# Normalisation in four groups, roots moved to GpSimd, and a new order of the first phase in an attention-and-FFN kernel

## The reference

```python
xn = (x - mean(x)) / sqrt(var(x) + 1e-5)              # by row; f32
Q, K, V = relu(xn @ Wq + bq), relu(xn @ Wk + bk), relu(xn @ Wv + bv)   # 16 heads of 8
s = layernorm(softmax(mask(Q @ K.T / sqrt(8))) @ V + xn) * gamma + beta # causal and key/query masks
xl = (xn - mu) * rsqrt(var(xn) + 1e-5) * ln_scale + ln_bias
xa = xl @ attn_w.T + attn_b + xn
h  = gelu(xa @ w1[e] + b1[e]);  eo = h @ w2[e] + b2[e]  # expert e fixed by the row's place
g = silu(gelu(eo @ next_w.T + next_b))
out = x + s * g
```

## Time and profile before

| | us |
|---|---|
| median of 3 runs | 456.26 |
| the 3 runs | 455.87, 456.26, 466.83 |
| the profiled execution's own time | 457.67 |
| its span, first to last instruction | 455.6 |
| VectorE busy in the span | 373.1 |
| TensorE busy in the span | 383.3 |
| GpSimd busy in the span | 179.1 |

### The profile page before, as it was taken

One profiled execution on the slowest core, in us unless ns is written; L12 is line 12 of the kernel. 1 busy time (PEld: TensorE's weight loads), 2 busy tenths in 40 slices (PEclk: granted clock), 3 DMA queues, 4 the chain that ended last, 5 costly groups with the idle time before them and its releaser, 6 DMA issues.

```text
span 455.6 us, 9692 instructions
## 1 busy us (share of the span) xinstructions
PE 383.3 (84%) x3541; PEld 249.3 (55%) x3541; DVE 373.1 (82%) x865; ACT 289.2 (63%) x580; POOL 179.1 (39%) x446
## 2 busy tenths in 40 slices
PE   0041899889999998899999999999999999999850
PEld 0021575457877775456656656665666566566420
DVE  5899388977778921899899999898999998989427
ACT  0122481278898884167777877877778778778740
POOL 9237000411111002311236547456556383565591
PEclk9997599999999999999999999999999999999995
DMA  8910030077644534723233342423332424340000
GB/s 238 316 52 1 0 100 0 0 170 160 156 112 115 139 98 116 128 57 86 81 90 79 82 109 73 118 63 105 92 96 64 129 56 113 79 110 27 4 24 23
DMA packets 31413, 41.72 MB, mean 92 GB/s; under 512 B 5910, under 2 KB 23686, under 8 KB 31366
## 3 DMA queue, kind: packets, MB, share of 16 engines
q1 hardware_dynamic: 31206, 41.08, 34.6%
q0 software_dynamic: 160, 0.03, 0.0%
HBM read 26.43 MB, written 11.02 MB: 82 GB/s over the span
## 4 chain that ended last, share of the span: by engine, by line
PE 43%; DVE 13%; issue 2%; ACT 1%; POOL 1%; DVEq 0%; ACTq 0%; POOLq 0%
PE banks L1152 15%; PE banks L1135 8%; DVE mx L951 8%; PE banks L1115 8%; PE banks L1117 5%; PE banks L1137 5%; DVE stats L996 2%; PE banks L1162 2%; DVE res L990 1%; ACT pt L1070 1%; PE banks L1124 0%; DVE res L977 0%; DVE res L980 0%; DVE mixed L981 0%; DVE aggr L1000 0%
## 5 line engine op out<-in xcount | busy, mean ns | idle before, releaser
L951 DVE TENSOR_REDUCE mx<-banks 128x1 f32<-128x512 f32 (+3 forms) x352 | 200.0, 633 | 19.9 <-PE banks L1117 18.2
L1070 ACT ACTIVATE pt<-banks 128x512 f32<-128x512 f32 x320 | 169.2, 601 | 44.2 <-PE banks L1137 36.7
L1152 PE MATMUL banks<-pt,vg 128*18 128x512 f32 (+3 forms) x1024 | 81.4, 436 | 0.7 <-ACT pt L1070 0.7
L1115 PE MATMUL banks<-k_own,q_own 76*128 76x384 bf16 (+2 forms) x192 | 48.4, 274 | 5.4 <-DVE mx L951 2.7
L1115 PE MATMUL banks<-w_room 76*128 76x384 bf16 (+2 forms) x192 | 48.1, 274 | 3.3 <-DVE mx L951 3.3
L842 POOL TENSOR_SCALAR mneg<-mx 128x16 f32<-128x16 f32 x32 | 8.1, 254 | 107.7 <-DVE mx L951 106.6
L1135 PE MATMUL banks<-w_room 76*128 76x384 bf16 (+2 forms) x192 | 47.5, 275 | 0.9 <-ACT pt L1070 0.5
L1135 PE MATMUL banks<-q_own,k_own 76*128 76x384 bf16 (+2 forms) x192 | 47.8, 274 | 0.0
L1152 PEld LDWEIGHTS banks<-pt,vg 128*18 128x18 f32 x1024 | 23.7, 97 | 43.8 <-issue 33.4
L1117 PE MATMUL banks<-k_own,q_own 124*128 124x128 bf16 x256 | 44.0, 219 | 0.0
L1117 PE MATMUL banks<-w_room 124*128 124x128 bf16 x256 | 43.8, 219 | 0.0
(11 more groups left out here) (175 smaller groups left out, 764.3 us busy)
## 6 DMA issues: line engine op xcount, KB each, us to landing
k_scratch<-parts SPq DMA_DIRECT2D x40, 128.0 KB, 2.4
k_own<-k_scratch SPq DMA_DIRECT2D x48, 96.0 KB
w_room<-k_scratch SPq DMA_DIRECT2D x48, 96.0 KB
q_scratch<-parts SPq DMA_DIRECT2D x24, 128.0 KB, 2.4
q_own<-q_scratch SPq DMA_DIRECT2D x32, 96.0 KB
w_room<-q_scratch SPq DMA_DIRECT2D x32, 96.0 KB
w_room<-in_w_dram SPq DMA_DIRECT2D x1, 2048.0 KB, 9.1
q_own<-q_scratch SPq DMA_DIRECT2D x16, 112.0 KB
```

Of the source, the lines that this page charges most:

```text
L951: dve.tensor_reduce(mx[:, u % 2, heads[0]:heads[-1] + 1, q], banks[:, S0 + slots[0] % SLOTS, 0:w * len(heads)].rearrange("p (h k) -> p h k ...
L1070: act.activation(pt[:, T * j:T * j + T], banks[:, bank(), :], ACT.Exp, scale=SCALE).then_inc(exp_done, 1)
L1115: mm(o[:, 0:w - P], qx[by][0:LIVE, g, h, P * q:P * q + P], kx[by][0:LIVE, g, h, 0:w - P], start=True, stop=True)
L1152: ins = mm(banks[32 * h:32 * h + VP, OT, P * k:T], vg[:, g, k, h, :], pt[:, KPLACE[k, h]:KPLACE[k, h] + n], start=(k == 0 and g % 2 == 0), ...
```

## The change

1. `GROUPS` becomes four groups of eight row tiles, which is two batches each. The DMAs of x stay two.
2. VectorE computes the roots of group 0 as before. For groups 1 to 3 it computes `statistics` (mean, variance, first seed of the root), GpSimd computes the roots (`first_roots`, 31 instructions of eight columns), and VectorE takes the inverse (`inverses`).
3. VectorE's order becomes: for each batch quotients, sums and the rests of the batch before; the statistics of groups 1, 2 and 3 follow the sums of batches 0, 2 and 4. The low parts of batch i-2 are now made inside `quotients(i)`, after its third instruction.
4. ScalarE makes the middle parts of batch i-1 at the start of its work on batch i, ahead of `split(i)`, and no longer between the GELUs. In the last batch they follow all the GELUs.
5. TensorE's 28 and 40 held products in batch 1 go. 22 are issued after the seeds of group 0 and before the first transposes, 8 after batch 0's projections.
6. GpSimd builds the bar rows of one 128-column tile, copies them three times over, and does so right after the bias rows. The ones of `v_all` are written in one column of nine only.

```diff
-GROUPS = ((0, 2 * TB), (2 * TB, NT - 2 * TB))
+LOADS = ((0, 2 * TB), (2 * TB, NT - 2 * TB))
+GROUPS = tuple((2 * TB * k, 2 * TB) for k in range(B // 2))
...
-HELD = (28, 40)
+HELD = (22, 8)
...
-                pool.memset(v_all[:, :, :], 1.0).then_inc(blank, 1)
+                pool.memset(v_all[:, :, :].rearrange("p n (h w) -> p n h w", w=VW)[:, :, :, DH], 1.0).then_inc(blank, 1)
...
-                    link(pool.affine_select(out=bar[:, :].rearrange("p (n t) -> p n t", t=P),
-                                            in_=bar[:, :].rearrange("p (n t) -> p n t", t=P),
-                                            compare_op=ALU.is_ge, fill=value, base=-k * sign,
-                                            pattern=[[0, TB], [sign, P]], channel_multiplier=-BLOCK * sign))
+                    link(pool.affine_select(out=bar[:, 0:P], in_=bar[:, 0:P], compare_op=ALU.is_ge, fill=value,
+                                            base=-k * sign, pattern=[[sign, P]], channel_multiplier=-BLOCK * sign))
 
                 def bar_rows():
 
-                    link(pool.memset(bar_k[:, :], BAR_KEYS[BLOCK]))
+                    link(pool.memset(bar_k[:, 0:P], BAR_KEYS[BLOCK]))
                     for k in range(BLOCK, 0, -1):
                         below(bar_k, k, BAR_KEYS[k - 1])
-                    link(pool.memset(bar_q[:, :], BAR_QUERIES[BLOCK - 1]))
+                    link(pool.memset(bar_q[:, 0:P], BAR_QUERIES[BLOCK - 1]))
                     for k in range(BLOCK - 1, -1, -1):
                         below(bar_q, k, BAR_QUERIES[k - 1] if k > 0 else 0.0)
                     below(bar_q, BLOCK - 1, 0.0, -1)
+                    for bar in (bar_k, bar_q):
+                        ins = pool.tensor_copy(bar[:, P:T].rearrange("p (n t) -> p n t", t=P),
+                                               bar[:, 0:P].unsqueeze(1).broadcast_to([BAR_ROWS, TB - 1, P]))
+                    link(ins)
                     pool.sem_inc(bars_ready, 1)
 
+                bar_rows()
...
+                def halves(x, hi, lo, u, w):
+
+                    link(pool.tensor_scalar(u, x, 4097.0, None, ALU.mult))
+                    link(tt(w, u, x, ALU.subtract))
+                    link(tt(hi, u, w, ALU.subtract))
+                    link(tt(lo, x, hi, ALU.subtract))
+
+                def first_roots(tok, group):
+
+                    at = slice(group[0], group[0] + group[1])
+                    a_, y_, t_, u_, s_, sh_, sl_, rem_ = (v[:, at] for v in (a, y, t, t3, s, sh, sl, rem))
+                    pool.wait_ge(first_seeds, tok.next(first_seeds))
+                    for _ in range(3):
+                        link(tt(t_, y_, y_, ALU.mult))
+                        link(tt(t_, t_, a_, ALU.mult))
+                        link(pool.tensor_scalar(t_, t_, -0.5, 1.5, ALU.mult, ALU.add))
+                        link(tt(y_, y_, t_, ALU.mult))
+                    link(tt(s_, a_, y_, ALU.mult))
+                    halves(s_, sh_, sl_, t_, u_)
+                    link(tt(t_, sh_, sh_, ALU.mult))
+                    link(tt(rem_, a_, t_, ALU.subtract))
+                    link(tt(t_, sh_, sl_, ALU.mult))
+                    link(tt(t_, t_, t_, ALU.add))
+                    link(tt(rem_, rem_, t_, ALU.subtract))
+                    link(tt(t_, sl_, sl_, ALU.mult))
+                    link(tt(rem_, rem_, t_, ALU.subtract))
+                    link(tt(t_, rem_, y_, ALU.mult))
+                    link(pool.tensor_scalar(t_, t_, 0.5, None, ALU.mult))
+                    link(tt(s_, s_, t_, ALU.add))
+                    halves(s_, sh_, sl_, t_, u_)
+                    pool.sem_inc(roots_ready, 1)
...
-                    if i == 0:
-                        second_roots(tok, GROUPS[0])
-                        bar_rows()
-                    if i == 2:
-                        second_roots(tok, GROUPS[1])
+                    if i % 2 == 0:
+                        second_roots(tok, GROUPS[i // 2])
                     totals(tok, i)
+                    if i % 2 == 0 and i + 2 < B:
+                        first_roots(tok, GROUPS[i // 2 + 1])
...
-                def quotients(i):
+                def inverses(tok, group):
+
+                    at = slice(group[0], group[0] + group[1])
+                    dve.wait_ge(roots_ready, tok.next(roots_ready))
+                    link(dve.reciprocal(r[:, at], s[:, at]))
+                    link(dve.tensor_scalar(nr[:, at], r[:, at], -1.0, None, ALU.mult))
+
+                def quotients(tok, i):
...
+                    if i > 1:
+                        lows(tok, i - 2)
...
+                def statistics(group):
+
+                    at = slice(group[0], group[0] + group[1])
+                    means(group)
+                    variances(group)
+                    rsqrt_newton(link, dve, y[:, at], t[:, at], a[:, at], 0)
+                    dve.sem_inc(first_seeds, 1)
+
                 tok = Tokens(dve)
                 dve.wait_ge(x_in[0], 16)
                 means(GROUPS[0])
                 variances(GROUPS[0])
                 roots(GROUPS[0])
-                quotients(0)
-                second_seeds(GROUPS[0])
-                sums(0)
-                quotients(1)
-                sums(1)
-                dve.wait_ge(x_in[1], 16)
-                rests(tok, 0)
-                means(GROUPS[1])
-                lows(tok, 0)
-                variances(GROUPS[1])
-                roots(GROUPS[1])
-                second_seeds(GROUPS[1])
-                rests(tok, 1)
-                for i in range(2, B):
-                    quotients(i)
-                    if i > 2:
+                for i in range(B):
+                    if i == 1:
+                        dve.wait_ge(x_in[1], 16)
+                        statistics(GROUPS[1])
+                    if i % 2 == 0:
+                        if i > 0:
+                            inverses(tok, GROUPS[i // 2])
+                        second_seeds(GROUPS[i // 2])
+                    quotients(tok, i)
+                    sums(i)
+                    if i > 0:
                         rests(tok, i - 1)
-                    sums(i)
-                    lows(tok, i - 1)
+                    if i % 2 == 0 and 0 < i < B - 2:
+                        statistics(GROUPS[i // 2 + 1])
                 masks()
+                lows(tok, B - 2)
                 rests(tok, B - 1)
                 lows(tok, B - 1)
...
+                def mids(tok, i):
+
+                    for o in range(2):
+                        act.wait_ge(rest_ready, tok.next(rest_ready))
+                        act.activation(parts[:, i % 2, o, 1, :], rest[:, o, :], ACT.Copy).then_inc(mid_ready, 1)
+
...
                     if i > 0:
+                        mids(tok, i - 1)
                         split(tok, i)
...
-
-                        act.wait_ge(rest_ready, tok.next(rest_ready))
-                        act.activation(parts[:, i % 2, h, 1, :], rest[:, h, :], ACT.Copy).then_inc(mid_ready, 1)
+                    if last:
+                        mids(tok, i)
                     if not last:
                         second_norm(tok, i + 1)
...
-                    if i == 0:
-                        pe.wait_ge(bias_ready, 1)
                     bias_first(0)
...
                 tok = Tokens(pe)
+                pe.wait_ge(bias_ready, 1)
+                pe.wait_ge(seeds_ready, 1)
+                hold(HELD[0])
                 normed(tok, 0)
                 pe.wait_ge(xnT_ready, tok.next(xnT_ready))
                 projections(tok, 0)
+                hold(HELD[1])
                 second_normed(tok, 0)
                 attn_product(tok, 0)
...
                     for h in range(2):
-                        if i == 1 and h == 1:
-                            hold(HELD[0])
                         pe.wait_ge(hid_ready, tok.next(hid_ready))
...
-                    if i == 1:
-                        hold(HELD[1])
```

More of the change, by code:

```diff
@@ L218, in build_program @@
         TRX, TRL, QB, KB, VB, XB, H0B = range(7)
-        x_in = [sem(f"x_in{k}") for k in range(len(GROUPS))]
+        x_in = [sem(f"x_in{k}") for k in range(len(LOADS))]
         rows_in, bias_ready = sem("rows_in"), sem("bias_ready")
@@ L228, in build_program @@
         lanes_ready, seeds_ready = sem("lanes_ready"), sem("seeds_ready")
+        first_seeds, roots_ready = sem("first_seeds"), sem("roots_ready")
         xl_ready = sem("xl_ready")
@@ L243, in build_program @@
             "mask_ready", "maskT_done", "maskT_ready", "mask_out"))
-        mean, var, a, y, t, s, sh, sl, r, nr, rem, v2, y2, t2 = (small[:, k, :] for k in range(14))
+        mean, var, a, y, t, s, sh, sl, r, nr, rem, v2, y2, t2, t3 = (small[:, k, :] for k in range(15))
         with nc.Block() as block:
@@ L249, in _ @@
             def _(sp):
-                for k, (t0, n) in enumerate(GROUPS):
+                for k, (t0, n) in enumerate(LOADS):
```

(6 more changed lines are left out.)

## The result

The changed kernel takes 485.11 us (median of 4 runs, 482.87 to 486.48), beside 460.17 of the kernel before in the same comparison (4 runs, 455.87 to 466.83). The ratio is 1.063, 95% interval 1.056 to 1.070; it sets the changed kernel against the two runs of the kernel before near 456 alone, since the other two (464.08 and 466.83) are of a second, slower kind that e9 takes up. It is slower, as forecast, but by more than twice as much: 468.2 was forecast, and the range ended at 478. The profiled execution took 482.87, with a span of 481.1, 25.5 more than the earlier trace rows.

The account below looks back on a forecast made before the run. It took phase 1's batch steps as deciding, with VectorE waiting at the low parts for ScalarE's middle parts. -8.3 + 10.2 + 7.5 + 2.5 = +11.9 gave 468.2 us from 456.26, range 458 to 478.

Parts of the forecast that it names:

- start to S(1): Phase 1 up to S(1), the start of batch 1's first transposes on TensorE: 52.4 against 60.75, -8.3 us.
- S(1) to S(7), stalls alone: Batches 1 to 7: VectorE waits at the low parts for ScalarE's middle parts, steps of 17.9 and 20.2; +10.2 us.
- S(1) to S(7), clock: TensorE idles 6 us before S(1), S(3), S(5), so batches there start at half clock; +7.5 us.
- end: End of phase 1: batch 7's later middle parts delay its first low part and SyncE's first store; +2.5 us.
- phase 2: The attention, after SyncE's last phase 1 DMA: taken as left as it is, no change forecast.
- all holes drop the clock: Rival, chance 0.14: phase 1's 4 us holes before full batches lower TensorE's clock too, +5.0 more, 473.2 us.
- The clock holds: Rival, chance 0.18: phase 1's 6 us holes are shorter or cost nothing; +4.4, 460.7 us.
- GpSimd's roots as slow: Rival, chance 0.11: first_roots at 0.47 an instruction takes 14.6 us, delaying S(1), S(3), S(5); +23, 479.3 us.
- The middle parts in time: Rival, chance 0.05: VectorE never stands still at the low parts in phase 1; -11.8, 444.5 us.
- The bounds: Ends set on phase 1's terms, putting the main forecast (chance 0.50) at 462 to 475 us.

Follow-up runs that it names:

- e9: Kernel before with 21 in place of 10 held products at the end of phase 1; 457.09 us (10 runs, 455.8 to 459.27).
- e6: e1 plus 16 to 30 held products ahead of each batch's transposes in phase 1; 466.44 us.
- e1: Changed kernel with 26 in place of 10 held products at the end of phase 1; 474.31 us.
- e7: Kernel before without the 10 held products at the end of phase 1; 466.38 us, ratio 1.011 to the kernel before.
- e13: Changed kernel with 26 end products and the low parts of batch i-2 moved from inside quotients(i) to behind sums(i); 449.44 us.
- e3: Kernel before with only the changed order of middle and low parts; 505.62 us, ratio 1.094.
- e12: Changed kernel with only the last batch's middle parts put back between its GELUs; 483.43 us.
- e4: Changed kernel with the first roots of groups 1 to 3 back on VectorE; 499.04 us.
- e2: Changed kernel with middle and low parts in their old order; 457.09 us (449.96, 452.47, 461.7 and 462.61).
- e15: e13's move, last middle parts between the GELUs, 10, 22, 22 held products before batches 1, 3, 5, 27 at the end; 446.62 us, ratio 0.975 to before.

## Why the prediction was wrong

Each step against its measurement, in us of the span:

| step | forecast | measured | |
|---|---|---|---|
| start to S(1) | -8.3 | -7.4 | GpSimd's roots begin at 38.28, not 37.6, and take 0.37 each, not 0.35; from totals to S 3.55, not 3.9 |
| S(1) to S(7), stalls alone | +10.2 | +14.5 (e6) | right in kind, too small |
| S(1) to S(7), clock | +7.5 | +5.1 (e1 less e6) | right in kind, too large |
| end | +2.5 | +3.4 | right to 1 us; 1.6 of it is the clock (e1 less e6) |
| phase 2 | 0 | +9.9 | **failed** |
| sum | +11.9 | +25.5 | |

**The step that failed** is the sentence "Phase 2 takes the rest of the 455.6 us and is left as it is, so I only ask when phase 1 ends." The code of phase 2 is left as it is; its clock is not. At the end the forecast put the middle and low parts of batch 7 later behind TensorE's last work, and it asked only what that does to SyncE's stores. SyncE's end moved from S(7) + 20.1 to S(7) + 23.5, and the attention's first product, which begins 0.8 after it, with it; TensorE's ten closing products moved by 1.6 alone, from S(7) + 16.1 to S(7) + 17.7. So the hole between them grew from 2.56 to 4.32. The prediction had the rule for it in hand, the fall after a pause, and used it for the holes inside phase 1 alone. e1 takes 10.8 us back by bridging this one hole, e7 makes the same loss in the kernel before, and with the term the forecast would have been 469.6 + 9.9 = 479.5 beside 482.87 of the profiled execution. The other terms miss by 3.7 in sum.

**The stalls at the lows** were right in place, releaser and pattern, and e13 and e3 show that they are the cause of what phase 1 lost. The steps S(1) to S(7) were forecast as 17.9 and 20.2 by turns, 2.5 more at 2, 4 and 6; measured 18.4, 20.7, 20.3, 20.7, 21.4, 19.8. With the clock held at 1.00 (e6) they are 18.4, 20.8, 18.4, 20.8, 19.6, 18.4, 4.4 more in sum than the stalls alone were forecast to give. About half a us of it stands in every step, and 1.2 more in the step to S(6): in e6 it is 4.3 us from totals to S at batch 4 and 5.5 at batch 6, where the totals run beside the long instructions of quotients(7), and 3.9 was taken. The idle times are longer than the forecast 4.0 partly because VectorE arrives earlier (at batch 2 at S + 0.1 and not at S + 1.3, with GpSimd and not VectorE setting S(1)), partly by the clock.

**The clock in phase 1** has nearly the right total for partly wrong reasons. The forecast let it fall before S(1), S(3) and S(5), 7.5 us, and hold at the shorter holes. Removing the falls takes 7.9 off the median (e6 against e1), and 6.7 off phase 1 in the profiles: 5.1 between S(1) and S(7), and 1.6 at the end. But it was at 0.50 for some us at the start of six batches, behind holes of 4.42 to 5.58, and held only before S(1), where the hole was 2.78: 1.00 from 50 to 66. So the rival "all holes drop the clock" (0.14) was right on the place for all but one. The Trainium skill, "TensorE: Matmul & The Clock Gate", section on HAM oscillation, says that each burst after such a wait starts cold; six rows of seven agree, with the 2.78 us hole as the exception.

That this hole was short is itself an accident of the clock. In the profile of after the clock had fallen to 0.50 in the middle of batch 0 already, at about 38.7, and the slow products ran on into the hole. The profile of e12, whose TensorE instructions up to S(1) are the same, has no fall there, and a hole of 5.72 with the fall behind it. Timeline of PE, the first products with w1 of batch 0 in after, then in e12 and its S(1):

```profile
41.61 5.52 PE L754 MATMUL banks<-xaT,w_room 128*128 128x256 f32 x16 [0.78 <-ACT xaT L603]
...
40.52 3.72 PE L755 MATMUL banks<-xaT,w_room 128*128 128x256 f32 x16 [0.78 <-ACT xaT L603]
...
53.41 1.12 PE L686 MATMUL banks<-ident,xl_st 128*128 128x128 f32 x4 [5.72 <-ACT xl_st L585]
```

S(1) is 53.36 in the one and 53.41 in the other, so this fall cost nothing there. It came with no idle time of TensorE over 1.23 us since its first product (1.23, 0.69, 0.84 and 0.87).

**Luck.** Inside phase 1 the stalls were 4.3 us more than forecast and the clock between S(1) and S(7) 2.4 us less; that the two sum to +19.6 beside the forecast +17.7 is in part such luck. It changes nothing in the step that failed.

**The rivals.** The clock holds (0.18): refuted, the six falls are in the trace. GpSimd's roots as slow (0.11): refuted by 0.37 and by e4; the exclusive lock of "SBUF — State Buffer", section "Who interferes with whom", in the Trainium skill, which would have given 0.57 each, does not show beside VectorE's sets of four, where they took 0.31. The middle parts in time (0.05): they came at S(1) + 5.3, exactly where ScalarE's order put them. e13 is in effect that rival's kernel, and it gave part of the gain that the rival priced: S(1) to S(7) took 99.4, where before had 101.8 and the rival 95.8.

**The bounds.** They took in unknowns of phase 1, and none of phase 2. The range was too narrow by a whole term, not by the size of one.

**Still open.** Why the clock stays at 0.50 for some 26 us at the start of phase 2, with TensorE busy throughout, when behind the six holes of phase 1 it came back within 3 to 5 us of a batch's start. The products there are other ones (76 or 124 rows and outputs of 128 to 512), and that was not varied. Nor is it known what decides at holes near 2.5 us: at 2.45 it fell, at 2.56 it held in the profiles of before and e2, whose runs come out at both levels. The length of the one hole is not all that decides: the fall in batch 0 stands behind much shorter ones, and in the profiles of the ten kernels with after's start it shows at 38.7 in two (after, e1), at 31 in three (e2, e13, e15), and not at all in five. The two levels of the runs were seen with a profile at one of them only, so that the upper level of before is this fall rests on its size, on the mean clocks of the runs, and on e9.

## What to carry to other kernels

- A wait costs what is queued behind it. Ask of each moved wait when its producer runs, and in whose queue; here the same low parts cost 25 us inside the quotients and nearly nothing behind the sums of the same batch.
- A phase that is not edited can still be changed by what reaches it: look at the idle time of each engine at the border, before and as forecast, and ask what state it hands over. For TensorE that is the clock. Here held products had to reach nearly up to the next real one: 19, which ended 2.45 us ahead of it, gave 455.5, and 27, 0.45 us ahead, gave 446.6.
- When the runs of one kernel fall into two groups a fixed amount apart, look for a term that is there or not (here 8 to 10 us), and compare the phases of a profile at each level. An edit that closes the gap in question, as e9, tells whether it is that term.

## What the hardware showed that was not expected

- The price of one fall of the clock was 8.5 to 10 us at the start of phase 2 (272.9 or 281.4 to 282.9), for holes from 2.45 to 4.81 us, and did not grow with the hole. All falls of phase 1 together cost 7.9, and the one in batch 0 nothing.
- The clock fell in batch 0 of the changed kernel at 38.7 with no idle time of TensorE over 1.23 us before it, and in other profiles with the same start at 31 or not at all.
- GpSimd's 128x8 instructions took 0.28 us from start to start with nothing in their way, 0.31 beside VectorE's sets of four, and 0.85 beside its two-input instructions on 512 columns, against 0.20 on VectorE. A chain of 31 was still worth 14 us there, because it runs beside VectorE's own work.
